# Repeating the tokens for the experts by DMA in place of TensorE and ScalarE, in an attention and mixture-of-experts block

## The reference, cut to what matters

```python
t = _to_tokens(x)                                   # (8, 4096, 32)
n = (t - mean(t)) / sqrt(var(t) + 1e-5)             # over the 32 channels
router_probs = softmax(n @ router_w + router_b)     # 8 experts
top_p, top_i = top_k(router_probs, 2)
top_p = top_p / sum(top_p)
expert_out = einsum('bnd,edc->bnec', n, expert_w) + expert_b
t = t + einsum('bnk,bnkc->bnc', top_p, take_along_axis(expert_out, top_i[..., None], axis=2))
```

## Time and profile before

| what | value |
|---|---|
| median of 3 runs | 448.45 us (447.75 to 449.42) |
| the profiled execution's own time | 449.4 us |
| its span | 447.6 us |
| mean granted clock of TensorE | 0.95 |
| TensorE busy | 387.8 us, 87% |
| VectorE busy | 343.4 us, 77% |
| ScalarE busy | 281.2 us, 63% |
| POOL busy | 160.2 us, 36% |
| DMA | 12.99 MB, mean 29 GB/s |

### The profile page before, as it was taken

How to read it: one execution, slowest core, us unless ns; L and a number is a source line. 1 busy time by engine, 2 the same in 40 slices (tenths; PEclk the granted TensorE clock), 3 DMA queues, 4 the chain that set the end, 5 groups by cost and what they waited for, 6 DMA issues and landing times.

```text
span 447.6 us, 11786 instructions
## 1 busy us (share of the span) xinstructions
PE 387.8 (87%) x4932; PEld 189.9 (42%) x4932; DVE 343.4 (77%) x432; ACT 281.2 (63%) x484; POOL 160.2 (36%) x187
## 2 busy tenths in 40 slices
PE   3788479999999999999999998884889788698995
PEld 1233235656666656566556565641222222122221
DVE  0289667989888879998989799993346885689775
ACT  2744327787878797778787976545456466344651
POOL 7600000112112111685451116865332335435743
PEclk9999687999999999999999999997799899769999
DMA  8500000000000000000001000000002100200311
GB/s 318 215 0 0 3 0 1 3 1 3 3 4 2 2 3 3 1 3 3 1 11 41 3 3 1 3 1 0 0 26 74 46 23 23 72 24 25 94 49 70
DMA packets 5811, 12.99 MB, mean 29 GB/s; under 512 B 640, under 2 KB 2688, under 8 KB 5376
## 3 DMA queue, kind: packets, MB, share of 16 engines
q1 hardware_dynamic: 5328, 10.49, 7.0%
q10 hardware_dynamic: 432, 1.77, 1.0%
HBM read 5.96 MB, written 4.19 MB: 23 GB/s over the span
## 4 chain that ended last, share of the span: by engine, by line
PE 64%; DVE 16%; ACT 8%; issue 6%; POOL 4%; DMA 2%; POOLq 0%; DVEq 0%; ACTq 0%
PE psum L521 12%; PE psum L538 8%; PE psum L392 6%; PE psum L508 6%; PE psum L641 4%; PE psum L664 4%; PE psum L546 4%; PE psum L483 4%; PE psum L478 4%; PE psum L674 3%; PE psum L492 3%; PE psum L412 2%; DVE neg_max L1035 2%; DVE window_work L1038 2%; ACT squares L424 2%
## 5 line engine op out<-in xcount | busy, mean ns | idle before, releaser
L278 POOL TENSOR_TENSOR o_norm<-o_tok,o_rden 128x128 f32<-128x128 f32 x64 | 25.3, 416 | 192.5 <-DVE o_rden L1048 192.5
L521 PE MATMUL psum<-weights_sb,window_work 128*128 128x128 f32 x512 | 82.3, 284 | 7.3 <-DVE window_work L1038 4.7
L803 ACT ACTIVATE probs<-psum 128x512 f32<-128x512 f32 x128 | 74.8, 595 | 20.0 <-PE psum L521 17.9
L1038 DVE TENSOR_TENSOR window_work<-psum,neg_max 128x1024 f32<-128x1024 f32 x64 | 78.4, 1225 | 2.2
L1035 DVE TENSOR_REDUCE neg_max<-psum 128x16 f32<-128x1024 f32 x64 | 76.9, 1201 | 3.2 <-PE psum L508 3.2
L521 PEld LDWEIGHTS psum<-weights_sb,window_work 128*128 128x128 f32 x512 | 57.8, 142 | 48.9 <-issue 28.1
L538 PE MATMUL psum<-probs,v_cols 128*32 128x64 f32 x2048 | 54.8, 225 | 0.3 <-DVE o_tok L1046 0.3
L918 ACT ACTIVATE stage<-psum 128x512 f32<-128x512 f32 x64 | 34.4, 594 | 23.7 <-PE psum L641 23.7
L538 PEld LDWEIGHTS psum<-probs,v_cols 128*32 128x32 f32 x2048 | 34.8, 109 | 28.6 <-issue 24.5
L641 PE MATMUL psum<-act_all,centre_rep 32*128 32x512 f32 x128 | 36.3, 676 | 11.7 <-ACT squares L424 7.5
L787 ACT ACTIVATE stage<-k_sb,weights_sb 128x512 f32<-128x512 f32 x64 | 44.1, 720 | 0.0
(11 more groups left out here) (115 smaller groups left out, 624.1 us busy)
## 6 DMA issues: line engine op xcount, KB each, us to landing
out<-out_sb SPq DMA_DIRECT2D x16, 256.0 KB, 2.0
stage<-in_x SPq DMA_DIRECT2D x3, 1024.0 KB, 13.3
gate_rows<-gate_parts SPq DMA_DIRECT2D x16, 128.0 KB, 2.9
stage<-in_x SPq DMA_DIRECT2D x2, 512.0 KB, 5.3
weights_sb<-weights ACTq DMA_DIRECT2D x1, 875.5 KB, 9.5
gate_f<-gate_sel ACTq DMA_DIRECT2D x1, 512.0 KB, 12.7
weights_sb<-weights ACTq DMA_DIRECT2D x1, 337.5 KB, 5.6
```

The lines of the kernel that those rows point to most:

```text
L521: last = nc.tensor.transpose(bank[TURN_BANKS[v % 2]][:, b * P:b * P + P], heads.rearrange("p h k -> p (h k)"), const["c_ident"][:, :])
L803: nc.scalar.activation(probs[:, w % 4, :], bank[TURN_BANKS[w % 2]][:, :], ACT.Exp).then_inc(exp_done, 1)
L1038: nc.vector.tensor_tensor(shifted_unit[:, unit % 2, :, :, :], t, m_t.unsqueeze(3).to_broadcast([P, IMG, HEADS, TOK]), ALU.add).then_inc(sh ...
```

## The change

The repeats are made by DMA on SP's queue: for each chunk and image, four transfers that copy the 32 partitions of the image in `act_all` to the four blocks of `x_rep`, sixteen transfers of 64 KB for a chunk, counted by one semaphore for each slot. They copy the tokens as they are. The centring goes into the weights: one more matmul multiplies the expert weights by the centring matrix, once. `replicate`, `keep_tokens` and `centre_rep` go. In SP's order, half of chunk 0 and chunk 1 are repeated as soon as their tokens are there, chunk 2 after the scores of chunk 14, the rest of chunk 0 and chunk 3 after those of chunk 15, and chunk c + 3 ahead of the gate moves and the store of chunk c. The last steps of quad 1's gates move behind the first products of chunk 0, on POOL, ScalarE and VectorE. The second normalisation of chunks 8 to 15 runs two chunks at a time in the second halves, in banks 0 and 1.

```diff
@@ allocations
-        centre_rep = sb("centre_rep", [P, P])
+        we_centred = sb("we_centred", [P, 2, C])
-        rep_ps = sem("rep_ps")
-        rep_done = sem("rep_done")
+        reps_in = [sem(f"reps_in{k}") for k in range(SLOTS)]
@@ SP
+            def repeat_tokens(c, images=range(IMG)):
+                sp.wait_ge(x2_done, c + 1 + X2)
+                if c >= SLOTS:
+                    sp.wait_ge(y_step, (c - SLOTS) * 2 + 2)
+                elif c >= 2:
+                    sp.wait_ge(score_ps, (CHUNKS - SLOTS + c) * 2 + 2)
+                elif images[0] == 0 and c == 0:
+                    sp.wait_ge(score_ps, CHUNKS * 2)
+                for b in images:
+                    for e in range(4):
+                        sp.dma_start(x_rep[C * e:C * e + C, c % SLOTS, b, :],
+                                     act_all[C * b:C * b + C, c * CHUNK:c * CHUNK + CHUNK]
+                                     ).then_inc(reps_in[c % SLOTS], 16)
+
+            repeat_tokens(0, range(2, IMG))
+            repeat_tokens(1)
             sp.wait_ge(filled, 4)
             move_gates(0)
+            repeat_tokens(2)
+            repeat_tokens(0, range(2))
             for c in range(CHUNKS):
+                if c + 3 < CHUNKS:
+                    repeat_tokens(c + 3)
                 if c % QUAD == 2 and c // QUAD + 1 < QUADS:
                     move_gates(c // QUAD + 1)
                 sp.wait_ge(summed, c + 1)
@@ POOL
             early(CHUNKS, 0)
-            early(CHUNKS, 1)
-            early(CHUNKS + 1, 0)
...
-                    pool.wait_ge(rep_done, c * IMG + IMG)
+                    pool.wait_ge(reps_in[c % SLOTS], (c // SLOTS + 1) * 16 * 16)
...
                     scale(c, eh)
+                    if h == 0:
+                        early(CHUNKS, 1)
+                    if h == 1:
+                        early(CHUNKS + 1, 0)
@@ TensorE
-            nc.tensor.matmul(bank[7][:, 0:2 * P], regroup[:, :], sel_sum[:, :],
-                             start=True, stop=True).then_inc(gate_sel_ps, 1)
+            nc.tensor.matmul(bank[7][:, 0:2 * P], regroup[:, :], sel_sum[:, :], start=True, stop=True)
+            nc.tensor.matmul(bank[7][:, 2 * P:2 * P + 2 * C], const["c_centre"][:, :],
+                             const["c_we"].rearrange("p a n -> p (a n)"), start=True, stop=True
+                             ).then_inc(gate_sel_ps, 1)
...
-                    last = nc.tensor.matmul(bank[6 + c % 2][32 * b:32 * b + 32, :], const["c_we"][:, eh, :],
+                    last = nc.tensor.matmul(bank[6 + c % 2][32 * b:32 * b + 32, :], we_centred[:, eh, :],
...
             def side(c, eh):
-                quad, h = c // QUAD + 2, c % QUAD * 2 + eh
-                ahead = c + REP_FIRST
-                if ahead < CHUNKS:
...
-                    replicate(ahead, (2 * eh, 2 * eh + 1), 0)
+                quad, k = c // QUAD + 2, c % QUAD
+                if eh == 1 and quad < QUADS and k < 3:
+                    pe.wait_ge(x2_done, CHUNKS + X2)
+                    if k == 0:
+                        pe.wait_ge(ln2["std_ready"], quad + ONE)
+                        pe.wait_ge(raw_done, quad)
+                    if k < 2:
+                        centre(pe, ln2, quad, 2 * k, tokens)
+                        centre(pe, ln2, quad, 2 * k + 1, tokens)
+                    else:
+                        variances(pe, ln2, quad, at=0)
+                        router(quad, at=1)
...
             pe.wait_ge(shifted_done, CHUNKS * 4)
-            replicate(0, range(IMG), 2)
             weigh(CHUNKS - 1, 1, NW - 2)
             weigh(CHUNKS - 1, 1, NW - 1)
-            pe.wait_ge(rep_done, IMG)
-            replicate(1, range(IMG), 2)
             project(CHUNKS - 1, at=OUT_BANK)
@@ ScalarE
-            keep_tokens(0, range(IMG), 2)
-            early_gates(CHUNKS, 1)
-            keep_tokens(1, range(IMG), 2)
-            early_gates(CHUNKS + 1, 0)
...
-                    if c + REP_FIRST < CHUNKS:
-                        keep_tokens(c + REP_FIRST, (2 * eh, 2 * eh + 1), 0)
-                    if quad < QUADS:
+                    if (c, eh) == (0, 0):
+                        early_gates(CHUNKS, 1)
+                    if (c, eh) == (0, 1):
+                        early_gates(CHUNKS + 1, 0)
+                    if eh == 1 and quad < QUADS:
                         if h < QUAD:
-                            square(act, ln2, quad, h, centred, banks=(SHARED,))
-                        elif h == 4:
+                            square(act, ln2, quad, h - 1, centred)
+                            square(act, ln2, quad, h, centred)
+                        elif h == 5:
                             token_deviations(quad)
-                        elif h == 5:
-                            keep_logits(quad)
+                            keep_logits(quad, at=1)
@@ VectorE
-            for b in range(IMG):
-                rows = slice(C * b, C * b + C)
-                nc.vector.tensor_copy(centre_rep[rows, :].rearrange("p (e c) -> p e c", e=IMG),
-                                      const["c_centre"][rows, rows].unsqueeze(1).to_broadcast([C, IMG, C]))
...
             dve.wait_ge(gate_sel_ps, 1)
+            nc.vector.tensor_copy(we_centred[:, :, :].rearrange("p a n -> p (a n)"),
+                                  bank[7][:, 2 * P:2 * P + 2 * C])
             nc.vector.tensor_copy(gate_sel[:, :], bank[7][:, 0:2 * P]).then_inc(gate_sel_ready, 1)
...
             divide(CHUNKS - 1, 1)
-            early(CHUNKS, 1)
             turn_back(CHUNKS - 1, 0)
...
-                dve.wait_ge(rep_done, c * IMG + IMG)
+                dve.wait_ge(reps_in[c % SLOTS], (c // SLOTS + 1) * 16 * 16)
...
+                    if (c, eh) == (0, 0):
+                        early(CHUNKS, 1)
                     steps(c, 2 * eh)
```

More of the change, by code:

```diff
@@ L186, in metaformer_block @@
         EARLY = 2
-        REP_FIRST = 2
         def wait_past(engine, s, n):
@@ L588, in chunk, with router @@
                         weigh(*at, back - 1)
-            def router(quad):
+            def router(quad, at=SHARED):
                 pe.wait_ge(ln2["squared"], quad * QUAD + (QUAD + XC))
                 for j in range(QUAD):
-                    at = (quad * QUAD + j) * CHUNK
-                    last = nc.tensor.matmul(bank[SHARED][32 * j:32 * j + 32, :], const["c_router"][:, 0, 0:C],
-                                            centred[:, at:at + CHUNK], start=True, stop=True)
+                    cols_at = (quad * QUAD + j) * CHUNK
+                    last = nc.tensor.matmul(bank[at][32 * j:32 * j + 32, :], const["c_router"][:, 0, 0:C],
+                                            centred[:, cols_at:cols_at + CHUNK], start=True, stop=True)
                 last.then_inc(logits_ps, 1)
@@ L636, in _ @@
                 chunk(m, m % 2, final=(m == CHUNKS - 1))
[L637 to L643, removed]
             def gate_pair(c, eh, pair):
@@ L717, in _ @@
             pe.wait_ge(exp_done, CHUNKS * NW + EXP)
-            pe.wait_ge(rep_done, REP_FIRST * IMG)
             for c in range(CHUNKS):
@@ L731, in _ @@
                         bias(c)
-                    side_norm(c, eh)
             experts(CHUNKS - 1, 1)
@@ L820, in gate_exps, with keep_logits @@
                 nc.scalar.activation(small[:, e_gap, :], small[:, gap, :], ACT.Exp).then_inc(gate_exp, 1)
-            def keep_logits(quad):
+            def keep_logits(quad, at=SHARED):
                 act.wait_ge(logits_ps, quad + 1)
                 wait_past(act, gate_step, (quad - 1) * GATE_OPS + (3 + ONE) if quad >= 1 else 0)
-                nc.scalar.activation(raw_logits[:, :], bank[SHARED][:, :], ACT.Copy).then_inc(raw_done, 1)
+                nc.scalar.activation(raw_logits[:, :], bank[at][:, :], ACT.Copy).then_inc(raw_done, 1)
             def gate_copies(quad, step):
@@ L911, in copy_gates @@
                 nc.scalar.activation(gate_copy[eh][:, :], bank[2][:, :], ACT.Copy).then_inc(gate_copied, 1)
-            def keep_tokens(c, images, first_bank):
-                act.wait_ge(rep_ps, c + 1 if c < REP_FIRST else c * 2 + (images[0] // 2 + 1 - REP_FIRST))
-                wait_past(act, y_step, (c - SLOTS) * 2 + 2)
-                for b in images:
-                    nc.scalar.activation(x_rep[:, c % SLOTS, b, :], bank[first_bank + b - images[0]][:, :], ACT.Copy
-                                         ).then_inc(rep_done, 1)
             exps(CHUNKS - 1, NW - 2)
             exps(CHUNKS - 1, NW - 1)
-            keep_tokens(0, range(IMG), 2)
-            early_gates(CHUNKS, 1)
-            keep_tokens(1, range(IMG), 2)
-            early_gates(CHUNKS + 1, 0)
             late_act = {}
```

17 lines of the change are left out of this document (removed).

## The result

The changed kernel takes 468.61 us (median of 4 runs, 468.23 to 470.87) against 448.57 for the kernel before (also of 4, 447.75 to 449.42): the ratio is 1.0457, with a 95% interval of 1.0418 to 1.0495. It is slower by 20 us. The forecast was 427, and the measured time lies above its range. It is within a microsecond of the 469.5 that rival A gave, to which I had given 0.19; A had worked that number out at 0.66 us an issue.

A forecast was written before the change was run, and what follows sets the result against it. TensorE leads in chunks 0 to 2 and nearly shares the lead with VectorE in 3 to 10. 447.6 + 0.3 - 4.6 - 9.5 - 7 - 0.5 = 426.3, with 0.85 427 us; range 416 to 462.

The forecast's parts named there:

- rival A: SP's queue binds, kernel slower: span 342 + 192a, a being us an issue; decides from a = 0.55; chance 0.19.
- the paragraph on SP's queue: Sixteen repeat issues a chunk at 0.39 us each, 6.6 us with the store, so SP keeps ahead in the middle.
- The entry: Ahead of chunk 0: early repeats gone and gate step 24 moved, first product at 308.0 for 312.65; gain 4.6 us.
- The centring: Expert weights centred on chip by one more matmul of 64 columns ahead of the first scores: +0.3 us.
- Chunks 0 to 2: TensorE's ring through ScalarE goes; 7.4 + 2 x 6.2 = 19.8 us for 29.8, gain 10 at best, 9.5 taken.
- Chunks 3 to 10: VectorE's 58.6 us of work, 3.9 waiting for POOL, 4 charged for the clock: 66.5 to 68 us, gain 7.
- The tail: Chunks 11 to 14: SP's order delays chunk 15 to 8.9 + 32a after chunk 11, 21.4 us for 21.9; gain 0.5.
- Rivals B to D: B: pieces at 0.45 to 0.54 us, 0.17; C: clock drops, 437, 0.06; D: chunks 0 to 10 unchanged, 446.5, 0.04.

The follow-up runs named there:

- The probes: Two runs of the kernel before with extra DMAs of several shapes, sizes and memory ends on SP's idle queue: 449.0 and 449.4 us.
- steps_moved: The kernel before with only gate steps 24 to 29 of quad 1 moved behind the first products of chunk 0: 443.49 us for 449.05.
- half_count: The changed kernel with two of the four repeat transfers of each image left out, 8 issues a chunk: 425.42 us, ratio 0.9456 to before.
- merged: The changed kernel with one transfer per image and chunk, 32 partitions onto 128, in place of four, same bytes: 424.21 us, ratio 0.9475 to before.
- tiny_pieces: The changed kernel with the same 256 repeat transfers, each of 16 columns (2 KB) instead of 512 (64 KB): 467.95 us, ratio 1.0447 to before.

## Why the prediction was wrong, point by point

**The step that failed** is the price in the paragraph on SP's queue: "The repeats are plain, 32 rows of 2 KB, a quarter of the store's rows, so I take 0.39". It was 0.633. I had both ends, 0.39 and 0.66, and chose between them by an idea of what an issue's price hangs on, namely rows and split dimensions. The probes show that it hangs on neither; the choice took the row that looked most alike and not the one with the same two kinds of memory at its ends. The row that spoke for the right value, a plain store at 0.60 behind four moves, I quoted and gave to the rival. The step that hangs on this price fails with it, "At 6.6 against 8.3 us a chunk SP keeps ahead in the middle": sixteen repeats and a store took 10.7 us (362.73 to 373.46 in SP's timeline), more than the 8.3, and the queue fell behind.

**The sum of rival A** was right as worked out: 342 + 192a is 463.5 at the measured 0.633. The span was 466.8. Two terms were off in it and cancel: store 0 came at 315.1, not 317.9 (-2.8), and the stores inside cost 0.63, not 0.39 (+2.9). What is left is mostly the long issues among the repeats, which add some 4.4 us over the twelve sets (the longest issue is 1.912); the last landing took 1.5 and not 2.4. That the 469.5 came so close is in part luck: it rests on 0.66, and at the measured price the sum gives 464.4 for the time, 4 us short.

**The chances.** With the two ends known, 0.55 as break-even and two of three rows at 0.60 or more, 0.19 for A was too little. The upper end of the range, 462, was cut inside A's own case. Its lower end, 416, doesn't follow from the terms named for it: 427 less 1.0, 4 and 1.6 (32 issues at 0.34 for 0.39) is 420.5.

**The entry** was 6.2 better for 4.6 forecast. Of this steps_moved shows 4.06 (312.65 to 308.59), for 4.0 expected. The rest is the early repeats' going and some 0.6 us at the start of the attention; its shares weren't measured apart.

**The centring** was given +0.3. The new matmul has a union of 0.43 us on TensorE, of which part overlaps; yet the scores behind it start earlier than before (63.40 for 64.04), since the prologue as a whole is about a microsecond earlier. It can't have cost more than its own 0.43.

**Chunks 0 to 2** took 17.3 for 20.3 forecast: the gain of 12.5 is larger than 9.5. Of the 3.0 between them 1.2 is chunk 0, which took 6.2 and not 7.4, and 1.3 are chunks 1 and 2, which took 5.6 and 5.4 and not 6.2; the rest is the half microsecond that I had held back. Chunk 0 has luck in it. It was forecast to start half-clocked, and in this trace its granted clock was 0.95; in half_count, with the same work on TensorE, it was 0.57 and chunk 0 took 8.4:

```profile
306.42:312.64 6.22, 5.33 (x26) 1.49 (x29) 4.13 (x6) 4.31 (x9) 5.52 (x6) 0.95 0.19 45
```

```profile
306.50:314.95 8.45, 8.31 (x26) 2.04 (x29) 4.26 (x7) 4.53 (x9) 6.17 (x6) 0.57 0.00 0
```

**Chunks 3 to 10** can't be judged in the changed kernel, whose queue covers them. In merged, with the queue out of the way, they take 67.5, inside the 66.5 to 68 given, with the clock at 0.82. The terms are right too: 59.1 us of VectorE's work for 58.6, 3.7 of waiting for POOL's step for 3.9, and 4.7 of waiting for gate matmuls where I had charged 4 for the clock.

**The tail** was forecast as 8.9 + 32a, so 29.2 at 0.633; it took 46.8. The reason: at chunk 11's start the queue was already far behind, and the gate move of quad 3 didn't wait for POOL's step but for SP to reach it, at 430.70, 20.1 us into chunk 11 and not 3.1. The formula holds only where SP waits for POOL. In merged it is 21.4, more than VectorE's 17.6, as the gates of quad 3 come late there too; its chain shows 2.5 us of gate transfer between POOL's step and TensorE.

**Rivals B to D.** Transport isn't the bound at 64 KB (tiny_pieces). The clock did fall, to 0.76 and 0.71 in the long stretches, but it doesn't explain the loss: TensorE is busy only 56% and 44% there and waits for the queue, and merged, at 0.82 with nearly the same work, keeps to the forecast in chunks 3 to 10. The repeats had been on the path, as half_count and merged show, so D falls.

## What to carry to other kernels

Count the issues of a queue, not only their bytes: transfer count times the price of an issue, with the store and all else of that queue added, against the time of a stage. Take the price from a row with the same kinds of memory at both ends and with a neighbour right ahead; a lone store to DRAM understates it nearly by half (0.336 for 0.591). Where work moves off an engine to DMA, one transfer that repeats its source over more partitions, with the weights laid out to match, did in four issues what sixteen could not, and a long wait for one transfer in a full queue says only where in the list it stands.

## What the runs showed of the hardware that I had not expected

An issue of an on-chip copy costs its queue 0.59 us in a row at 2 KB and at 256 KB alike, and one with DRAM at either end 0.42 to 0.44; a store to DRAM right behind an on-chip copy pays 0.58, though alone it takes 0.33 to 0.36. Two queues issue side by side at these prices. Among sixteen repeats there is now and then one of 1.7 to 1.9 us, and in tiny_pieces too (up to 1.988 at 2 KB), so the bytes don't make it; the cause of these pauses is open. An issue of 32 partitions onto 128 took 1.2 us in a row in the probe, at 159 GB/s with the DMA engines 0.84 busy, where 128 partitions onto 128 reached 291.
